# Cross attention: a time for each of eight places in the order of maximum, scores and values, in place of a pattern of two slots

## The reference

```python
q = (query @ Wq.T).reshape(B, Nq, H, Dh).transpose(0, 2, 1, 3)     # H = 16 heads of Dh = 16
k = (key @ Wk.T).reshape(B, Nk, H, Dh).transpose(0, 2, 1, 3)       # Nk = 4096
v = (value @ Wv.T).reshape(B, Nk, H, Dh).transpose(0, 2, 1, 3)
sim = jnp.einsum('bhqd,bhkd->bhqk', q, k) * SCALE
attn = jax.nn.softmax(sim, axis=-1)
out = jnp.einsum('bhqk,bhkd->bhqd', attn, v)
x = x + out.transpose(0, 2, 1, 3).reshape(B, Nq, C) @ Wo.T + bo
```

## Time and profile before

| | |
|---|---|
| time, median of 3 runs | 4958.12 us (4954.34 to 4961.64) |
| the profiled execution: its time, its span | 4963.8 us, 4961.9 us |
| mean granted clock of TensorE, share of full speed | 0.967 |
| busy over the span: TensorE, VectorE, ScalarE, GpSimd | 89%, 65%, 58%, 38% |
| first cross attention, about 0 to 1048 us: TensorE, VectorE, ScalarE busy | 909.24, 755.40, 648.11 us |
| second cross attention, about 3237 to 4285 us | 917.17, 750.75, 642.10 us |

### The profile page before, as it was taken

The page is one execution under the profiler, slowest core; times in us unless marked ns, Lnnn a source line. Parts: engine busy times, 40 slices in busy tenths (PEclk is TensorE's granted clock), DMA queues, the critical chain, the costliest instruction groups (busy, mean ns, idle before and its releaser), DMA issues. The chain is left out here.

```text
span 4961.9 us, 85570 instructions
## 1 busy us (share of the span) xinstructions
PE 4427.0 (89%) x31624; PEld 3025.6 (61%) x31624; DVE 3249.4 (65%) x7542; ACT 2896.0 (58%) x5798; POOL 1872.0 (38%) x1876
## 2 busy tenths in 40 slices
PE   5899998989789999999999999859999999669999
PEld 3555555547556666666676666635555555358888
DVE  5677777767565666656656666356777777575555
ACT  2666666668556666666666666426666666523332
POOL 2223222215564545445545444223222222035554
PEclk8999999989899999999999999979999999879999
DMA  5655555500110010100001000056555555011110
GB/s 138 131 103 104 104 113 102 94 24 1 56 39 6 23 45 13 54 15 26 33 14 53 16 32 6 13 126 129 108 103 104 110 109 90 12 53 49 49 48 19
DMA packets 189931, 305.60 MB, mean 62 GB/s; under 512 B 19736, under 2 KB 109752, under 8 KB 187832
## 3 DMA queue, kind: packets, MB, share of 16 engines
q1 hardware_dynamic: 189520, 300.13, 27.3%
HBM read 215.81 MB, written 73.40 MB: 58 GB/s over the span
## 5 line engine op out<-in xcount | busy, mean ns | idle before, releaser
L707 DVE TENSOR_REDUCE xa_m_part<-xa_ring 128x1 f32<-128x512 f32 x2048 | 1319.1, 686 | 506.3 <-PE xa_ring L856 491.0
L633 ACT ACTIVATE xa_ex<-xa_sc 128x1024 f32<-128x1024 f32 x1024 | 991.6, 1022 | 114.2 <-PE xa_sc L844 99.0
L856 PE MATMUL xa_ring<-xa_ks,xa_q_base 48*128 48x512 f32 x2048 | 517.8, 498 | 185.6 <-DVE xa_m_part L707 129.4
L870 PE MATMUL xa_pv<-xa_ex,xa_vs 128*17 128x256 f32 x8192 | 547.8, 385 | 1.3 <-issue 1.3
L856 PEld LDWEIGHTS xa_ring<-xa_ks,xa_q_base 48*128 48x128 f32 x2048 | 201.4, 185 | 517.2 <-DVE xa_m_part L707 432.9
L1036 ACT ACTIVATE lt_p<-lt_bank,lt_stat,lt_rq 128x128 f32<-128x128 f32 (+1 forms) x768 | 365.6, 482 | 215.4 <-DVE lt_stat L1006 210.1
L1570 POOL TENSOR_TENSOR lt_r_qk<-lt_r_qk,lt_t_rot 128x512 f32<-128x512 f32 x192 | 243.2, 1267 | 611.1 <-DVE lt_t_rot L1686 606.1
L844 PE MATMUL xa_sc<-xa_q_base,xa_ks 50*128 50x256 f32 x4096 | 423.0, 302 | 26.4 <-ACT xa_k L605 5.2
L844 PEld LDWEIGHTS xa_sc<-xa_q_base,xa_ks 50*128 50x128 f32 x4096 | 346.8, 187 | 117.5 <-ACT xa_vs L620 24.1
L1023 POOL TENSOR_SCALAR lt_p<-lt_p,lt_stat 128x192 f32<-128x192 f32 x384 | 335.0, 876 | 197.8 <-DVE lt_stat L1013 197.8
L2412 PE MATMUL moe_bank<-moe_xp,moe_wp 128*128 128x512 f32 x1536 | 373.3, 392 | 5.9 <-POOL moe_wp L2240 4.2
(11 more groups left out here) (281 smaller groups left out, 8755.1 us busy)
## 6 DMA issues: line engine op xcount, KB each, us to landing
xa_ks<-keys SPq DMA_DIRECT2D x384, 256.0 KB, 9.1
keys<-xa_kp SPq DMA_DIRECT2D x128, 512.0 KB, 3.8
xa_cx<-in_ctx_t SPq DMA_DIRECT2D x64, 512.0 KB, 4.9
lt_wqk<-in_lt_wqkv SPq DMA_DIRECT2D x6, 2048.0 KB, 8.4
lt_w<-in_lt_w SPq DMA_DIRECT2D x6, 1536.0 KB, 6.2
xa_q_base<-xa_m_rows SPq DMA_DIRECT2D x512, 2.0 KB
moe_w<-in_moe_wg SPq DMA_DIRECT2D x64, 128.0 KB, 2.2
moe_w<-in_moe_wu SPq DMA_DIRECT2D x64, 128.0 KB, 2.3
```

What stands on the lines that cost most here:

```text
L633: act.activation(x.ex[:, n % x.NE, :, :], x.sc[n % 2][:, :, :], ACT.Exp).then_inc(*x.ex_done.one())
L707: dve.tensor_reduce(x.m_part[:, i % 2, qt, h, ch:ch + 1], x.bank(n + odd), AX.X, ALU.max).then_inc(*x.dve_out.one())
L856: pe.matmul(x.bank(n + odd), x.q_base[rows, pair, b * S + qt * P:b * S + (qt + 1) * P], x.ks[unit % x.NU][rows, pair % 4, ch * 512:(ch + 1 ...
L870: mm = pe.matmul(x.pv[32 * j:32 * j + x.VW, :], x.vs[:, i % x.NV, kt, 4 * g + j, :], x.ex[:, n % x.NE, 2 * (j % 2) + j // 2, :], start=(kt ...
```

## The change

The list is no longer made in stretches of two slots. Each step gets a time in slots, and the list is the steps sorted by it. For each of the eight places of a slot in its group there are three constants: when its maximum comes (less the lead of 18 slots), its scores and its values. `max_rows`, `place_max`, `gather`, `combine`, `stack_k`, the two jobs of a group, `query`, `stack_q`, `turn_out` and `project_out` have one time each. The number of steps, what each does and every wait are as before; the order in which each engine meets them is new.

```diff
+    MAX = (-0.14, 0.15, 1.75, 3.12, 3.52, 4.23, 5.93, 7.06)
+    SCORES = (0.99, 1.18, 1.66, 2.08, 4.37, 5.31, 5.93, 6.02)
+    WEIGH = (3.43, 3.87, 5.21, 5.84, 6.88, 7.26, 8.56, 9.49)
+    JOBS = (0.44, 4.14)
+    PLACE_MAX, MAX_ROWS, GATHER, COMBINE, STACK = 7.37, -7.37, 12.16, 14.47, 26.48
+    QUERY, TURN_OUT = 2.4, 2.05
...
-        jobs = iter(self.filling())
-        for t in range(-self.LEAD, total + 20, 2):
-            top = t + self.LEAD
-            quad, at = divmod(t, 8)
-            side = []
-            if at == 0 and 0 <= quad + 1 < 4 * self.ITEMS:
-                side.append(("max_rows", quad + 1))
-            if at == 4 and 1 <= quad <= 4 * self.ITEMS:
-                side.append(("gather", quad - 1))
...
-            scores = [("scores", n) for n in (t, t + 1) if 0 <= n < total]
-            first, second = ([("max", top)], [("max", top + 1)]) if top < total else ([], [])
-            out += first + side + second + scores if side else first + scores + second
-            if second and top % 8 == 6:
-                out.append(("place_max", top // 8))
-            for n in (t - 2, t - 1):
-                if 0 <= n < total:
-                    out.append(("weigh", n))
-            unit, at_u = divmod(t + 30, 16)
-            if at_u == 0 and 1 <= unit < 2 * self.ITEMS:
-                out.append(("stack_k", unit))
...
+        for n in range(total):
+            i, place = divmod(n, 8)
+            at(8 * i + self.MAX[place] - lead, ("max", n))
+            at(8 * i + self.SCORES[place], ("scores", n))
+            at(8 * i + self.WEIGH[place], ("weigh", n))
+            if place == 7:
+                at(8 * i + self.PLACE_MAX - lead, ("place_max", i))
+                at(8 * i + self.MAX_ROWS, ("max_rows", i))
+                at(8 * i + self.GATHER, ("gather", i))
+                b, kb = divmod(i // 4, self.NKB)
+                if kb == self.NKB - 1:
+                    at(8 * i + self.COMBINE, ("combine", b, i % 4))
+        for unit in range(1, 2 * self.ITEMS):
+            at(16 * unit - self.STACK, ("stack_k", unit))
+        for n, job in enumerate(self.filling()):
+            early = lead // 2
+            slot = 2 * n - lead + 0.1 if n < early else 8 * ((n - early) // 2) + self.JOBS[(n - early) % 2]
+            at(slot, job)
...
+        return out + [step for _, _, step in sorted(timed)]
```

More of the change, by code:

```diff
@@ L382, in steps, with at @@
-        return out
+        lead, timed = self.LEAD, []
+        def at(slot, *steps):
+            timed.extend((slot, len(timed) + m, step) for m, step in enumerate(steps))
+        for n in range(total):
[10 more added lines that the diff above has]
+                    at(8 * i + self.COMBINE, ("combine", b, i % 4))
@@ new lines, in steps @@
+        for unit in range(1, 2 * self.ITEMS):
[4 more added lines that the diff above has]
+            at(slot, job)
+            if job[0] == "value" and job[2] % 2 == 1:
+                m = 2 * (job[1] + 1) + job[2] // 2
+                at(slot, *[("split", m)] * (m < 2 * self.ITEMS), *[("ctx", m + 2)] * (m + 2 < 2 * self.ITEMS))
@@ L384, in count_uses @@
+        for b in range(B):
+            if b:
+                for mt in range(2):
+                    at(12 * b - 2 + 4 * mt + self.QUERY, ("query", b, mt))
+                at(12 * b + 6 + self.QUERY, ("stack_q", b))
+            at(batch * (b + 1) + 14 + self.TURN_OUT, ("turn_out", b))
+            at(batch * (b + 1) + 18 + self.TURN_OUT, ("project_out", b))
+        return out + [step for _, _, step in sorted(timed)]
     def count_uses(self):
```

## The result

The kernel is slower: 5073.31 us median (5067.81 to 5082.78, 4 runs) against 4959.88 us (4954.34 to 4962.29, 4 runs) for the kernel before on the same chip, a ratio of 1.0232 (95% interval 1.0212 to 1.0252). That is 113.4 us more; 5002 was forecast, with 5050 as the upper end.

The account below looks back on a forecast made before the run. The prediction took TensorE as nearly the bound (busy 917 of 1048 us). It added 7 us for the order and 38 for late keys, +45 us, forecasting 5002 us against the median, 0.9% slower; range 4925 to 5050 us.

Parts of the forecast that it names:

- Interval by interval: TensorE's distances between maxima in a group of eight slots, priced one by one: 14.69 us against 14.29, 0.40 more.
- free splitting: Rival: dear transitions on TensorE turn out at their lower bounds, a group is 14.13 us, time 4930 us; chance 0.22.
- ScalarE's falling behind: Rival: S3, the second job and S7 start late, a group is 0.3 us longer, time 5040 us; chance 0.12.
- Extras of a batch: Time in a batch beyond its sixteen groups (`combine`, `turn_out`, `project_out`, late place_max): 9.1 us taken down to 3.6.
- The order's part as a whole: The new order's price without late keys: a batch 0.9 us longer, +7 us over eight batches.
- I take 1.3 for each, +38 us: Wait of maximum M0 for stacked keys queued behind a key job's transfer on SyncE, over 30 late units.
- late units: Units whose stacked keys land after M0 is due: odd ones from 3 to 31, 15 in a stage, 30 in all.
- the upper bound of 3 us a unit: Most that late keys could cost (90 us), if the next group's key transfer gets in between.
- keys in time: Rival: the six key transfers land within 13.9 us or SyncE is sooner, the 38 us go, 4965 us; chance 0.16.

Follow-up runs that it names:

- experiment 1: The changed kernel with only `stack_k` put back ahead of the group's second job (27.9 in place of 26.48): 4971.74 us, ratio 1.0020.
- experiment 5: As experiment 1, with only the last `combine` of each batch moved 3.85 slots later: 4952.21 us, ratio 0.9986 to the kernel before.
- experiment 2: The kernel before the change, with only `stack_k` moved behind the second job's transfer: 5048.86 us, ratio 1.0178.

## Why the prediction was wrong

The direction and the mechanism of the larger part were right; its size was not, and the time fell 23 us beyond the range. By its own steps:

- **Interval by interval: right, within 0.1 us each.** The forecast was 3.20, 1.37, 1.37, 1.42, 2.66, 1.88, 1.37, 1.42, sum 14.69. The trace after has 3.25, 1.28, 1.37, 1.42, 2.56, 1.86, 1.44 and 1.41 in the ordinary group from 455.66 us, sum 14.59 by these and 14.60 by its two ends; ordinary groups are 14.53 to 14.65. M3 to M4 undercuts the 1.37 that was taken for the least distance: M4 waits for nothing there. `gather` to S4 is 0.31 and not 0.37, and scores ahead of a value step take 0.43 to 0.44 and not 0.34. The rival of free splitting (14.13) is out. ScalarE's falling behind is out as well, though its cover at S3 was not there: S3 waits 0.17 for an exponential in the group shown above, and M4 to M5 is 1.38 all the same. The scores' waits for exponentials are 20.7 us in 108 small waits, not 0.3 a group.
- **Extras of a batch, 9.1 down to 3.6: right in an undisturbed batch, wrong at two places.** Sixteen groups of the second stage in experiment 1 (3677.65 to 3915.61, all at the higher clock) take 237.96 us, where 238.6 was forecast and 237.74 stood before. The order's part as a whole, measured by experiment 1, is +10.6 us where +7 was forecast, but that near agreement hides two errors. `combine` was priced at 0.4 us from the row, with VectorE alone in view; the last `combine` of a batch meets GpSimd's split of the context, and moving it is worth some 17 to 20 us by experiment 5. Everything else together is then 9.7 us faster than before, where 7 slower was forecast. The traces of before and of experiment 5 show where. One group near each stage's start (136.11 and 3369.68 us before) takes 24.04 and 22.58 us before, where odd scores wait 4.98 and 3.40 for the copy of a key job's result, and 16.15 and 16.08 in experiment 5, without such a wait. Against it the first two groups of the stages are 10.4 us longer together; the `combine` groups are 4.7 shorter. The prediction left the stages' starts out.
- **The failed step: "I take 1.3 for each, +38 us".** The stacked keys cost 102.8 us. The number of late units was nearly right (30 forecast, 28 found: no key job stands ahead of unit 31, as the stage's jobs have ended), and so were the place (M0), the queueing behind the key job's transfer (4.92 us from job to first issue, 4.91 forecast) and the landing (15.3 to 16.0 from the first issue in the 26 units, 15.5 forecast). Two things were mis-sized. The wait is 1.94 and not 1.3: the working itself gave 1.6, which was shaded down for slower groups that didn't come, and the groups are 0.1 shorter, so M0 is due sooner. With the longer waits at unit 3 that makes 61.5 us in 28 waits (59.3 net of the stages' start) instead of 38. And a stalled TensorE was priced at the time that it stands, with nothing for its clock afterwards: in 20 of 26 groups it ran at half clock behind the stall, 2.24 us more each (18.82 less 16.58), 45 us with nothing in the forecast against it. This is what put the time outside the range; even the upper bound of 3 us a unit was a bound on waiting alone, and it was not carried into the range in full.
- **The rival "keys in time"** did not come, but it was nearly right about the rest: with the keys ahead the kernel is at 1.0020 (1.0012 to 1.0029), at the edge of what a measurement tells from no change.

By sum: 59 (waits) + 44 (the rest of experiment 1's 102.8, clock behind them) + 20 (`combine` against the split) - 10 (everything else) = 113. The second and the last term are what the others leave, so the sum is a division and no check of its own; the check is the count by groups under experiment 2. The division of the 102.8 between waiting and clock is from traces, not from a run that holds the clock.

## What to carry to other kernels

When a step of a DMA queue is moved past another, subtract the new landing from the new due time for each use, and look at what TensorE does behind a wait: here one of about 2 us cost about twice its length. A list of times hands every step to one sort, so after it is made, look at each queue for what a transfer now stands behind, and at each VectorE operation with two SBUF inputs for what GpSimd is doing meanwhile. A schedule that is slow by a few per cent can be one constant from one that isn't: here `STACK` alone made 1.0232 into 1.0020. The same way of making the list, with other times for nearly every step, gave 0.9781.

## What the runs showed of the hardware

- A TensorE wait of 1.6 to 2.3 us was followed, in 20 of 26 cases, by matmuls at the 1.2 GHz level for some 3 to 7 us, and the same was seen where VectorE was what it waited for. A group with both is 17.6 to 19.8 us long, with the wait alone 16.3 to 16.7, with neither 14.6.
- VectorE's addition of 128 x 512 from two SBUF tiles: 0.69 us by itself, 2.72 while GpSimd works on its 128 x 1024 split; the small product L742 0.29 and 0.90.
- A value step standing alone costs 0.55 to 0.56 to the next step, a pair 0.99. Scores alone take 0.34 ahead of a maximum and 0.43 to 0.44 ahead of a value step. Scores behind `max_rows` or `gather` follow after 0.31. The prediction had 0.55, 0.99, 0.34 for scores in either place, and 0.31 and 0.37.
